# Expert products of a mixture-of-experts layer: one fp32 matmul each, or three products of rounded high and low parts

## The reference

```
flat = hidden_states                                  # 2048 x 256
top_w, top_i = top_k(softmax(flat @ router_w + router_bias), 2)
for e in range(15):
    y = silu(flat @ expert_gate_w[e]) * (flat @ expert_up_w[e]) @ expert_down_w[e]
    routed = routed + combine[:, e:e + 1] * y         # gate, up 256x128, down 128x256
gate = conv(flat, conv_w)                             # 3 taps, 256 -> 128
shared = silu(gate) * (flat @ shared_up_w) @ shared_down_w
```

## Time and profile before

| | |
|---|---|
| time, median of 3 runs | 785.16 us (784.21 to 786.78) |
| profiled execution | 784.08 us, of it the span 782.3 us |
| PE busy | 634.2 us (81%) |
| DVE busy | 587.0 us (75%) |
| POOL busy | 477.9 us (61%) |
| ACT busy | 443.1 us (57%) |
| mean granted TensorE clock | 0.903 of full speed |

### The profile page before, as it was taken

The page is one execution under the profiler, slowest core; times in us unless marked ns, Lnnn a source line. Parts: engine busy times, 40 slices in busy tenths (PEclk is TensorE's granted clock), DMA queues, the critical chain, the costliest instruction groups (busy, mean ns, idle before and its releaser), DMA issues. The chain is left out here.

```text
span 782.3 us, 10673 instructions
## 1 busy us (share of the span) xinstructions
PE 634.2 (81%) x3106; PEld 397.6 (51%) x3106; DVE 587.0 (75%) x990; ACT 443.1 (57%) x784; POOL 477.9 (61%) x386
## 2 busy tenths in 40 slices
PE   4589875997699965577966999999999898799940
PEld 2133212352133410043535999998989764688830
DVE  5886888699998999999987667587787645444317
ACT  2678698686986888757735354544454310344420
POOL 4168689788998999999946232323354155056650
PEclk9899986999779996596997999999999999999985
DMA  7083044425144445844003142343222169455418
GB/s 202 17 202 87 22 109 108 102 53 132 38 108 108 109 108 117 231 107 108 1 9 125 43 138 68 114 136 101 78 89 70 48 195 319 105 159 145 125 42 294
DMA packets 58294, 87.39 MB, mean 112 GB/s; under 512 B 14101, under 2 KB 43224, under 8 KB 58238
## 3 DMA queue, kind: packets, MB, share of 16 engines
q1 hardware_dynamic: 42686, 67.24, 33.3%
q10 hardware_dynamic: 11616, 10.76, 4.4%
q0 software_dynamic: 3936, 8.72, 3.2%
HBM read 36.54 MB, written 18.66 MB: 71 GB/s over the span
## 5 line engine op out<-in xcount | busy, mean ns | idle before, releaser
L277 POOL TENSOR_TENSOR b_in<-rep,b_rep 128x1024 f32<-128x1024 f32 x128 | 299.3, 2357 | 36.0 <-DVE h L515 29.0
L515 DVE TENSOR_TENSOR_SCAN h<-ps,hlast,b_in 128x512 f32<-128x512 f32 x256 | 306.1, 1260 | 15.1 <-ACT ps L419 8.1
L419 ACT ACTIVATE ps<-rep,neg_a 128x512 f32<-128x512 f32 x256 | 171.3, 685 | 49.4 <-DVE h L515 45.6
L701 PE MATMUL ps<-h,pick 128*32 128x512 f32 x512 | 81.9, 717 | 50.3 <-DVE h L515 49.9
L997 POOL DMA_INDIRECT rows_by_token<-yt,yrow x46 | 44.8, 975 | 53.9 <-DVE yrow L1354 26.8
L554 PE MATMUL ps<-xnT,w_in 128*128 128x512 f32 x128 | 69.5, 690 | 9.8 <-ACT xnT L327 4.1
L1150 DVE TENSOR_TENSOR p_lo<-ps,p_hi 128x512 fp32r<-128x512 f32 x64 | 35.4, 599 | 43.5 <-ACT p_hi L1008 43.4
L701 PEld LDWEIGHTS ps<-h,pick 128*32 128x32 f32 x512 | 10.7, 115 | 99.6 <-DVE h L515 90.9
L1392 PE MATMUL ps<-v_hi,p_hi 128*128 128x256 f32 x208 | 59.7, 287 | 1.2 <-DVE x_res L1253 1.2
L1392 PE MATMUL ps<-v_hi,p_lo 128*128 128x256 f32 x208 | 58.3, 280 | 0.0
L1392 PE MATMUL ps<-v_lo,p_hi 128*128 128x256 f32 x208 | 58.1, 279 | 0.0
(11 more groups left out here) (239 smaller groups left out, 1361.7 us busy)
## 6 DMA issues: line engine op xcount, KB each, us to landing
rep<-dt_u SPq DMA_DIRECT2D x252, 128.0 KB, 2.3
mask_sb<-in_mask_BxSxS_ik_dram SPq DMA_DIRECT2D x16, 800.5 KB, 4.3
xt<-rows_by_expert SPq DMA_DIRECT2D x46, 129.0 KB, 2.3
rows_by_token<-pad ACTq DMA_DIRECT2D x4, 1024.0 KB, 5.0
yb<-rows_by_token SPq DMA_DIRECT2D x4, 512.0 KB, 5.0
yb<-rows_by_token ACTq DMA_DIRECT2D x4, 512.0 KB, 5.9
x_res<-in_x_dram SPq DMA_DIRECT2D x1, 1536.0 KB, 8.7
c_raw<-in_ctx_dram SPq DMA_DIRECT2D x1, 1536.0 KB
```

Source lines behind the costliest of these rows:

```text
L277: pool.tensor_tensor(b_in[:, (t - 1) % NB:(t - 1) % NB + 2, :], u_rep[:, n % 2, j - 1:j + 1, :], b_rep[q % 2][:, g, :].unsqueeze(1).to_bro ...
L419: act.activation(psA[:, t % NDA, :], dt_rep[:, n % 2, j, :], ACT.Exp, scale=neg_a[:, k:k + 1]).then_inc(exp_ready, 1)
L515: dve.tensor_tensor_scan(h[:, QC * (s % NH) + j, :], psA[:, t % NDA, :], b_in[:, t % NB, :], hlast[:, k:k + 1], ALU.mult, ALU.add).then_in ...
L701: last = pe.matmul(psY[32 * j:32 * j + 32, :], pick[:, :], h[:, QC * (s % NH) + j, :], start=False, stop=(g == NG - 1))
```

## The change

Each fp32 product of an expert tile (gate with up, and down) is done as three fp32r matmuls of 256 columns by `products`. For that

- the 15 experts' weights are split once into `w_hi` (ACT copies, 3840, 3072 and 4608 columns, after silu(2), after that, and after silu(3)) and `w_lo` (differences: the first two groups on POOL behind its last scatter, the third on DVE behind `shared_add(3)`, ahead of `route_weights`),
- PE waits for the three low parts in the place of the weights' landing,
- T's result is split by ACT (`xT_hi`) and DVE (`xT_lo`), H's result as well (`hT_hi`, `hT_lo`), in each step,
- to make room, `xt`, `yt`, `cv`, `t1` and some more lie where the attention's context and values were; some semaphores are merged, with the same waits.

```diff
+W_GROUPS = ((0, 5), (5, 9), (9, 15))
...
+        def weights_low(eng, g):
+            a, b = W_GROUPS[g]
+            eng.wait_ge(whi_ready, g + 1)
+            eng.tensor_tensor(w_lo[:, a:b, :], w_all[:, a:b, :], w_hi[:, a:b, :].bitcast(F32), ALU.subtract).then_inc(wlo_ready, 1)
...
+            weights_low(pool, 0)
+            weights_low(pool, 1)
...
-            for c in range(2, NCH):
-                silu(c)
+            def weights_high(g):
+                a, b = W_GROUPS[g]
+                act.wait_ge(w_exp_in[g], 16 * 3 * (b - a))
+                act.activation(w_hi[:, a:b, :], w_all[:, a:b, :], ACT.Copy).then_inc(whi_ready, 1)
+
+            silu(2)
+            weights_high(0)
+            weights_high(1)
+            silu(3)
+            weights_high(2)
             route_exp(NCH - 1)
...
-                    act.activation(xT[:, s % 2, :], psX[s % 2], ACT.Copy).then_inc(xT_ready, 1)
+                    act.activation(xT_hi[:, s % 2, :], psX[s % 2], ACT.Copy).then_inc(xhi_ready, 1)
...
+                    act.activation(hT_hi[:, i % 2, :], psH[i % 2][:, 0:2 * P], ACT.Copy).then_inc(hhi_ready, 1)
...
             shared_add(3)
+            weights_low(dve, 2)
             route_weights(NCH - 1)
...
+                    dve.tensor_tensor(xT_lo[:, s % 2, :], psX[s % 2], xT_hi[:, s % 2, :].bitcast(F32), ALU.subtract).then_inc(xT_ready, 1)
...
-                    dve.tensor_copy(hT[:, i % 2, :], psH[i % 2][:, 0:2 * P]).then_inc(hT_ready, 1)
+                    dve.tensor_tensor(hT_lo[:, i % 2, :], psH[i % 2][:, 0:2 * P], hT_hi[:, i % 2, :].bitcast(F32), ALU.subtract).then_inc(hT_ready, 1)
...
-            pe.wait_ge(w_exp_in, 16 * 3 * NX)
+            pe.wait_ge(wlo_ready, len(W_GROUPS))
...
-                            last = pe.matmul(psG[i % 2][:, a * 2 * FI:(a + 1) * 2 * FI], xT[:, i % 2, cols],
-                                             w_all[:, ds(e, 1), wcols].rearrange("p a n -> p (a n)"), start=(k == 0), stop=(k == KE - 1))
+                            last = products(psG[i % 2][:, a * 2 * FI:(a + 1) * 2 * FI], (xT_hi[:, i % 2, cols], xT_lo[:, i % 2, cols]),
+                                            tuple(t[:, ds(e, 1), wcols].rearrange("p a n -> p (a n)") for t in (w_hi, w_lo)), k == 0, k == KE - 1)
```

More of the change, by code:

```diff
@@ L772, in attend_and_route @@
         sg, sh_raw = late
-        x3, xn3, xt, (xT, hT, sgt, ht, yt) = tail_bufs
+        x3, xn3, (xt, yt, cv, t1, cv_raw, done), (xT_hi, xT_lo, hT_hi, hT_lo, sgt, ht) = tail_bufs
         mv, rstd = stats
@@ L802, in attend_and_route @@
         with ExitStack() as second:
[L803 to L810, removed]
+            with ExitStack() as whole:
+                w_all = sb("w_exp", [P, NX, WE], F32, whole)
+            w_lo = sb("w_lo", [P, NX, WE], F32R, second)
+            with ExitStack() as last:
+                yb = sb("yb", [P, YB, HALF, 2 * DM], F32, last)
+            w_hi = sb("w_hi", [P, NX, WE], F32R, second)
         bank = [ps[:, n * BANK:(n + 1) * BANK] for n in range(8)]
@@ L835, in attend_and_route @@
         rows_filled, rows_in, pads_in = sem("rows_filled"), sem("rows_in"), sem("pads_in")
-        w_exp_in = sem("w_exp_in")
+        w_exp_in = [sem(f"w_exp_in{i}") for i in range(len(W_GROUPS))]
+        whi_ready, wlo_ready, xhi_ready, hhi_ready = sem("whi_ready"), sem("wlo_ready"), sem("xhi_ready"), sem("hhi_ready")
         shared_in, cv_ps, cv_ready = sem("shared_in"), sem("cv_ps"), sem("cv_ready")
@@ L1615, in tile_step @@
                         rows = slice(a * P, (a + 1) * P)
-                        last = pe.matmul(psY[i % 2][:, a * DM:(a + 1) * DM], hT[:, i % 2, rows],
-                                         w_all[:, ds(e, 1), 2 * KE * FI:].rearrange("p a n -> p (a n)"), start=True, stop=True)
+                        last = products(psY[i % 2][:, a * DM:(a + 1) * DM], (hT_hi[:, i % 2, rows], hT_lo[:, i % 2, rows]),
+                                        tuple(t[:, ds(e, 1), 2 * KE * FI:].rearrange("p a n -> p (a n)") for t in (w_hi, w_lo)), True, True)
                     last.then_inc(y_ps, 1)
@@ L1660, in decoder_layer @@
             c_all, v_all = sb("c_all", [P, KE, SKP], F32, whole), sb("v_all", [P, KC, DM], F32, whole)
+        with ExitStack() as ffn:
+            cv, t1 = sb("cv", [P, KS, KE, FI], F32, ffn), sb("t1", [P, 2, BANK], F32, ffn)
+            cv_raw, done = sb("cv_raw", [P, DM, KS], F32, ffn), sb("done", [P, NTILE, NX], F32, ffn)
+            sb("spare", [P, (KE * SKP * 4 - 13024) // 4], F32, ffn)
+            xt, yt = sb("xt", [P, XT, 2, ROW], F32, ffn), sb("yt", [P, YT, 2, DM], F32, ffn)
+            own = (xt, yt, cv, t1, cv_raw, done)
         with ExitStack() as kept:
@@ L1704, in decoder_layer @@
         with ExitStack() as tail:
[L1705 to L1707 removed]
+            tile_bufs = (sb("xT_hi", [P, 2, KE * 2 * P], F32R, tail), sb("xT_lo", [P, 2, KE * 2 * P], F32R, tail),
+                         sb("hT_hi", [P, 2, 2 * P], F32R, tail), sb("hT_lo", [P, 2, 2 * P], F32R, tail),
+                         sb("sgt", [P, 2, 2, FI], F32, tail), sb("ht", [P, 2, 2, FI], F32, tail))
         x3 = sb("x3", [P, KE, KS - 1 + SEQ])
[L1709 removed]
         xn3 = sb("xn3", [P, NT, ROW])
         attend_and_route(nc, ins["mask_BxSxS2_ik1"], w_ffn, x_res, (mv2, rstd2), (pad, pad_made, r_w, r_b, lower, ones_b),
[L1712 removed]
+                         (mask_sb, bv, c_all, v_all, c_lo, v_lo, wqk, fold, xn2, q_bufs), (sg, sh_raw), (x3, xn3, own, tile_bufs),
                          (b_in, r_in), ident, (xs_dram, y_dram), ps, out)
```

46 lines of the change are left out of this document (26 added, 20 removed).

## The result

| | before | changed |
|---|---|---|
| median (range) of the runs, us | 785.69 (784.21 to 786.78) | 804.06 (802.20 to 805.24) |
| profiled execution: time, span, us | 784.08, 782.3 | 802.20, 800.5 |
| T(0), start | 673.26 | 683.49 |
| G(0), start | 676.31 | 686.10 |
| T(4) to T(22), 18 steps | 58.50 | 66.25 |

The ratio is 1.024, with an interval of 1.021 to 1.026: 18.4 us slower, where +7.9 was forecast (from the three runs of before known then, median 785.16; here there are four). In the profiled executions the difference is 18.1: +9.8 to G(0), -0.2 from G(0) to T(4), +7.75 in the 18 steps, +0.9 behind T(22).

The account below looks back on a forecast made before the run. PE's array bounds the kernel before, PE's sequencer the changed steps. Start +9.7, 18 steps -0.9, end -0.9 make +7.9 us: 792.0 on the profiled 784.08, 793 as median; range 786 to 799 (8 in 10).

Parts of the forecast that it names:

- The array's 2.78 us a step: PE's array in an expert step: six products at 0.353 us, T and H unchanged, 2.78 us instead of 3.26.
- The sequencer becomes the bound: Expert steps: PE's sequencer, at 3.2 us against the array's 2.78, sets the step, which stays about where it was.
- PE is busy 87% of the 18 steps: Sign in the expert steps: PE busy only some 87% of a 3.2 us step, idling for "issue".
- The added cost of a product, 0.12: PE's sequencer: REGISTER_ALU 0.035, a turn 0.058 and two more matmuls 0.03 add 0.12 us a product (0.08 to 0.144).
- The 0.058 of a plain turn: PE's sequencer between reads of expert numbers: some 0.058 us for each turn to the next instruction.
- The sequencer needs 3.2 us (2.96 to 3.36): PE's sequencer in a step: 2.5 us before plus 0.7 for the change, 3.2 us in all.
- -0.9 us in 18 steps: Steady expert steps: 18 x (3.2 - 3.25) = -0.9 us (-5.2 to +2.0).
- The step of 2.5 us that I took for a whole one: PE's sequencer before, between two EVENT_SEMAPHORE (684.3 to 686.8): a whole step of 2.5 us, leaving 0.75 of slack.
- slower still: Rival in the expert steps: reads slow when data moves or REGISTER_ALU exceeds 0.05; step 3.5 us, 798.5 us; chance 0.12.
- Start +9.7: Expert stage's start: PE waits for the last low part, DVE's held by POOL; G(0) at 686.0 instead of 676.3, +9.7 us.
- End -0.9: Last steps: the two array-bound steps after T(22) shorten by 0.47 each until POOL binds, -0.9 us (0 to -1).

Follow-up runs that it names:

- experiments 1: Changed kernel with the expert numbers of TensorE's tiles as constants, no table reads or register instructions between matmuls: 780.66 us, ratio 0.995.
- experiment 5: Changed kernel with PE's expert numbers read without the bounds test, everything computed: 782.93 us, ratio 1.000 to the kernel before.
- experiment 2: Kernel before the change with the expert numbers of TensorE's tiles as constants: 783.89 us, ratio 1.000.
- 4: Changed kernel with the weights' high and low parts in five pieces of three experts, all low parts on DVE: 789.83 us, ratio 1.007.
- experiment 3: Changed kernel with each of POOL's 46 tile scatters replaced by a one-element memset: 785.93 us, ratio 1.003.
- 12: Changed kernel with eight more one-element activations on ACT ahead of its tile loop: 795.29 us, kernel before 783.48.
- 8: Changed kernel with the weights in five pieces of three experts, first three low parts on POOL, last two on DVE: 792.74 us, kernel before 783.07.
- 13: Changed kernel with eight more one-element memsets on POOL behind its low parts: 795.44 us, kernel before 783.48.
- 17: Changed kernel with one more one-element activation on ACT ahead of its tile loop: 795.88 us, kernel before 781.91.
- 14: Changed kernel with ACT's high parts in five pieces, low parts left in three groups: 795.54 us, kernel before 783.48.
- 16: Changed kernel with eight more one-element memsets on DVE ahead of its tile loop: 794.59 us, kernel before 781.91.
- 18: Changed kernel with eight more one-element activations on ACT behind its tile loop: 792.92 us, kernel before 781.91.

## Why the prediction was wrong

Direction and mechanism held, and the size did not. Two things made it: the sequencer's step was sized too small, which the runs explain, and the stall was not foreseen, which they don't. By the prediction's own steps:

- **The array's 2.78 us a step: right.** 2.76 in experiments 1 and 5, with PE busy throughout.
- **"The sequencer becomes the bound": right**, shown by experiment 5 from the one side (take 0.57 us of sequencer time, gain 0.62 to 0.64) and by experiment 2 from the other (before, it had slack). Without the stall PE is busy 87% of the 18 steps (53.10 of 60.80 in 4), as the prediction said it would look. The added cost of a product, 0.12, measured 0.112, though its parts were off: REGISTER_ALU 0.032, and a turn with a matmul in it 0.078 to 0.081. (The 0.058 of a plain turn is right too, but follows from reads that start 0.649 apart and not from the rounded 0.6.)
- **"The sequencer needs 3.2 us (2.96 to 3.36)", so -0.9 us in 18 steps: the step that failed first.** It holds from T(3) to T(5), 3.15 and 3.12. From then on the pace is 3.38 to 3.40 with everything running, 60.8 to 61.1 us for 18: 2.5 more than before the change where I had 0.9 less. The three parts of the difference lie in the sequencer's records of experiments 3 and 12:
  - 0.11 is a fourth wait. PE waits for `yt` of two pairs before only once there is such a pair, ahead of D in step 5 and after. It holds the sequencer 0.051 and brings one more turn of 0.055. The step of 2.5 us that I took for a whole one in the earlier trace rows, 684.3 to 686.8, is the last without it; its line in the kernel before, and with the change but without scatters (3):

```profile
L1612 PEldq EVENT_SEMAPHORE  x18: 51/51/51, 688.2 to 743.4; - x18
```

```profile
L1637 PEldq EVENT_SEMAPHORE  x18: 51/51/51, 699.8 to 755.8; - x18
```

  - 0.10 to 0.12 are the two reads of expert numbers, which take longer while POOL scatters: 0.60 us a step together in 3, 0.70 to 0.72 in 4, 8, 12, 13 and 17. Singly they are never over 311 ns without scatters (3) and up to 571 with them (12):

```profile
L1594 PEldq TENSOR_LOAD <-tab_e x38: 296/298/311, 694.0 to 753.8; - x38
```

```profile
L1598 PEldq TENSOR_LOAD <-tab_e x36: 296/307/571, 695.8 to 754.3; - x36
```

  - 0.07 are turns that are now and then some 60 to 70 ns longer, with scatters and without. What makes them so is not settled.

  3.12 + 0.11 + 0.07 is the 3.29 of experiment 3 but for 0.01, and with the reads it is 3.40 to 3.42. The rival "slower still" had the reads' part, with 3.5 us; I had costed the sequencer from a quiet and incomplete step and put the bound of the range there as well.
- **"Start +9.7": right**, +9.8, and for the stated reason (4 and 8).
- **"End -0.9": about right without the stall** (37.8 us behind T(22) in 12, 38.9 before), and +0.9 with it.
- **The stall: not in the prediction at all, and the greater part of the miss.** 66.25 us in the first measurement, 67.2 to 68.1 on chip 6, 60.8 to 61.1 elsewhere: 5 to 7 us, and 1 to 3 more behind T(22).

With the pace at 3.40 the sum is 9.8 - 0.2 + 2.6 - 1.1 = +11.1, and the changed kernel with a few idle instructions more or its high parts in five pieces, where there is no stall, is 11.8, 12.0 and 12.1 us (12 to 14) and 12.7, 14.0 and 11.0 us (16 to 18) slower than the kernel before beside it. The forecast of +7.9 was some 4 us short of that, which its range, to +13.8, still held but for one of the six; the rest of the 18.4 is the stall, which put it outside.

What the stall is stays open. What is seen: SP, ACT and, for a shorter time, PE are held together; on SP and PE durations of 500 to 690 ns are followed by ones of 3 ns, which no instruction of that kind takes in the sixteen other traces; it came on chip 6 and in the first measurement and not on three other chips. Times of 3 ns look more like records written late than like work. The Trainium skill (NOTIFIC — the notification-queue block, Overflow: three behaviours, one of which stalls the engine) says that the block's internal path for an engine's records pushes back rather than losing one, and that its count of stalls would tell that it had throttled an engine. By it the stall could be the recording's, and a kernel with more instructions (11181 against 10673) might meet it sooner; but kernels of 11189 did not meet it on the other chips. No run here shows it: every time above comes from an execution with spans, and none was made without.

## What to carry to other kernels

When a change shortens what the array does and lengthens what the sequencer does, add up both, and add the sequencer's sum in a step in which everything else runs, not in a quiet one; check too that the step is a complete one, as the early steps of a pipeline lack some of its waits. A bounds test on a register value costs 0.28 us each time, and taking it away won 12 us here (782.9 in 5 against 795.3 in 12, on one chip), while in the kernel before even the absence of all register work won nothing (2). Don't put one long two-input SBUF operation on DVE and another on POOL: cut it into pieces and lay all of them into DVE's gaps. And when an edit without a task mends something, ask first whether the kernels that were compared ran on the same chip, and run the unaltered one beside them.

## What the runs showed that I had not expected

- The turns of PE's sequencer: FUSED_REGOPS 46 to 51 ns, REGISTER_ALU 32, a wait 51 when it is met, a table read some 300 when quiet, FUSED_REGOPS of the bounds test 151 and its assertion 18, some 58 ns between any two of the reads' instructions and some 80 where a matmul is issued between two. It decides a step of 18 matmuls.
- 17.1 us at the lower clock against 3.4 cost little, since PE waited in most of that stretch. What counts is how long it lasts behind G(0): 2.0 us of it or 5.3 make 8.02 or 9.09 us up to T(4).
- The stall: SP, ACT and briefly PE held together every 7.7 us on one chip (and in the first measurement), 5 to 7 us in 66; never on three other chips.
